# Convolutions of a wavelet block as split float32r products, with weights streamed in pages and shifted copies made by DMA

## What is computed

```python
def conv_block(x):                        # x: group-normalised, one channel per group
    LL, LH, HL, HH = dwt_haar(x)          # four bands of 64 x 64
    hf = concat([LH, HL, HH])             # 96 channels
    x1 = lrelu(conv5(lrelu(conv5(hf, w15)), w25))
    x2 = lrelu(conv3(lrelu(conv3(hf, w13)), w23))
    x3 = lrelu(conv2(lrelu(conv2(hf, w12)), w22))
    y = x1 + x2 + x3
    for w in (wd1, wd2, wd3):
        y = lrelu(conv3(y, w, dilation=2))
    phf = sigmoid(conv1(y, wca)) * hf
    z = batchnorm(conv3(concat([LL, phf]), wcb))
    return idwt_haar(z * sigmoid(z), conv1(phf, whf), HL, HH)

x = x + conv_block(gn(x))
x = x + codebook[argmin(distance(gn(x), codebook))]   # 512 codes of 32 channels
```

## Time and profile before

| | |
|---|---|
| median of 3 runs | 2165.28 us (2164.94 to 2166.05) |
| span of the profiled execution | 2164.4 us |
| TensorE busy, share of the span | 1984.8 us, 92% |
| VectorE busy | 1810.3 us, 84% |
| GpSimd busy (rough) | 1252.3 us, 58% |
| ScalarE busy | 1059.2 us, 49% |
| granted TensorE clock, mean | 0.951 of full speed |

### The profile page before, as it was taken

The page is one execution under the profiler, slowest core; times in us unless marked ns, Lnnn a source line. Parts: engine busy times, 40 slices in busy tenths (PEclk is TensorE's granted clock), DMA queues, the critical chain, the costliest instruction groups (busy, mean ns, idle before and its releaser), DMA issues. The chain is left out here.

```text
span 2164.4 us, 27115 instructions
## 1 busy us (share of the span) xinstructions
PE 1984.8 (92%) x5232; PEld 946.5 (44%) x5232; DVE 1810.3 (84%) x3979; ACT 1059.2 (49%) x2018; POOL 1252.3 (58%) x1299
## 2 busy tenths in 40 slices
PE   6999999999999999999999999999999999995653
PEld 3444455444544455444544445444544445442221
DVE  4122799988999799988999899988999889888996
ACT  5134645545555545546556454546455454543331
POOL 2001277654776377663776367673776457673876
PEclk9999999999999999999999999999999999995555
DMA  6000011111110112111111111111111011110111
GB/s 203 15 10 5 20 40 43 27 29 34 46 35 21 41 36 47 25 24 41 42 36 26 42 35 41 30 24 37 43 41 26 20 25 34 30 25 20 34 37 32
DMA packets 80459, 76.97 MB, mean 36 GB/s; under 512 B 29200, under 2 KB 62608, under 8 KB 80016
## 3 DMA queue, kind: packets, MB, share of 16 engines
q1 hardware_dynamic: 45776, 50.78, 8.3%
q0 software_dynamic: 32768, 16.84, 5.2%
q10 hardware_dynamic: 1728, 7.41, 0.9%
HBM read 41.36 MB, written 16.78 MB: 27 GB/s over the span
## 5 line engine op out<-in xcount | busy, mean ns | idle before, releaser
L1053 POOL DMA_INDIRECT vqc<-in_codebook,idx x1024 | 1000.9, 977 | 545.2 <-DVE idx L964 306.4
L542 PE MATMUL ring<-hf,w_sb 128*128 128x512 f32 x1824 | 888.5, 600 | 2.9 <-ACT hf L715 2.9
L487 PE MATMUL score<-cst,yst 98*128 98x512 f32 x1024 | 788.4, 777 | 83.8 <-DVE idx L964 54.8
L960 DVE MAX8 top<-score 128x8 f32<-128x512 f32 x1024 | 695.3, 684 | 74.7 <-PE score L487 63.8
L964 DVE FIND_INDEX8 idx<-top,score 128x8 uint32<-128x512 f32 x1024 | 704.2, 690 | 0.0
L666 ACT CAST yst<-bands 32x256 fp32r<-32x256 f32 x1024 | 411.3, 402 | 174.6 <-PE score L487 162.1
L542 PEld LDWEIGHTS ring<-hf,w_sb 128*128 128x128 f32 x1824 | 341.6, 191 | 316.9 <-issue 294.2
L487 PEld LDWEIGHTS score<-cst,yst 98*128 98x128 f32 x1024 | 204.0, 202 | 395.0 <-DVE idx L964 206.3
L542 PE MATMUL ring<-ha,w_sb 128*128 128x512 f32 x704 | 347.5, 598 | 5.1 <-DVE ha L853 4.6
L542 PE MATMUL ring<-hb,w_sb 128*128 128x512 f32 x544 | 262.6, 595 | 6.8 <-DVE hb L866 6.8
L627 ACT ACTIVATE z<-ring,prm 128x512 f32<-128x512 f32 x144 | 99.0, 688 | 273.3 <-PE ring L542 272.7
(11 more groups left out here) (101 smaller groups left out, 1276.8 us busy)
## 6 DMA issues: line engine op xcount, KB each, us to landing
xnat<-in_x SPq DMA_DIRECT2D x128, 128.0 KB, 2.7
yst<-yl SPq DMA_DIRECT2D x512, 32.0 KB
vqc<-in_codebook,idx POOLq DMA_INDIRECT x1024
out<-vqc SPq DMA_DIRECT2D x128, 128.0 KB
w_sb<-in_weights ACTq DMA_DIRECT2D x1, 1920.0 KB, 8.2
w_sb<-in_weights ACTq DMA_DIRECT2D x3, 384.0 KB, 12.8
w_sb<-in_weights ACTq DMA_DIRECT2D x1, 1152.0 KB, 15.6
w_sb<-in_weights ACTq DMA_DIRECT2D x1, 960.0 KB, 8.6
```

The source lines that it names most:

```text
L487: nc.tensor.matmul(score[BANK["tile", t]][:, :], yst[0:KST, j % 2, g, wp], cst[0:KST, :], start=True, stop=True).then_inc(s_tile, 1)
L542: t = nc.tensor.matmul(ring[g % RING][:, :, :], w_sb[:, SLOTS[n, m, kind, ky], :], own(source(n, m, kind), half, slice(PAD + di, PAD + di ...
L960: nc.vector.max(top8[:, t % 4, :], score[BANK["tile", t]][:, :]).then_inc(s_top, 1)
L1053: nc.gpsimd.indirect_dma_start(vqc[:, c % 2, w * CH:(w + 1) * CH], None, codebook[:, :], bass.IndirectOffsetOnAxis(idx[:, c % 2, k, 0:1], ...
```

## The change

1. Each product becomes three float32r matmuls. Weights and data are both held as a rounded part and the rest: `MAIN` is rounded by rounded, `WLOW` the rest of the weights by rounded data, `XLOW` rounded weights by the rest of the data. An image takes 678 of them instead of 226.
2. Both parts of 113 matrices don't fit, so they lie in DRAM (`wparts`) in 15 pages of at most 8 matrices (about 1 MB with both parts), and SyncE reads them into a ring of three pages in each round. In the first round they are made: SyncE reads a raw page, ScalarE rounds it, VectorE subtracts, SyncE stores it.
3. Each activation tile gets two parts. The leaky ReLU of w15, w13, w12 and wd1 to wd3 stays in `z`, and the sum behind w22 in `br`. ScalarE copies them rounded (14 copies a round, 128 x 512), and GpSimd subtracts to get the rest (14 subtractions, `split_low`). ScalarE's evacuation waits for VectorE's leaky ReLU in between, and for GpSimd's subtraction of two groups before. The bands are rounded by ScalarE (`normal_own`) with VectorE making the rest (`normal_low`, `ll_low`).
4. `attend` writes the weighted bands to `br`, after each half; ScalarE then scales and rounds (`weighted_high`, directly behind its evacuation of the group), and VectorE makes the rest (`weighted_low`).
5. All shifted copies (`edge`, `side`) are DMAs issued by SyncE, both parts in one DMA, two to four DMAs a copy. ScalarE's copies go.
6. The chunk of the next image is read with even and odd columns apart (runs of 128 bytes), and TensorE makes transpose and Haar transform in one, by four float32 matmuls of 256 columns against a matrix of signs. ScalarE copies to the bands and squares with a sum for the variance; VectorE's four additions and statistics per chunk go.
7. The plan counts 682 steps. `mean2` stands at step 36, `var2` at 60, `bias2` at 72; turns begin at step 84 and end 64 before the end; each of four places (behind w22, wd1, wd2, wd3) counts as 24 places, so that some five turns gather there. A gather is issued a tile later than before. SyncE walks the plan as the others do.

The diff's core:

```diff
-LEAD, REAR = 9, 16
+LEAD, FIRST_TURN, REAR = 36, 84, 64
+CHAIN = ("w22", "wd1", "wd2", "wd3")
+CHAIN_STEPS = 24
+PG, NR = 8, 3
...
+def unit_steps(unit):
+    steps, rest = [], list(unit)
+    while rest:
+        page = PAGE[rest[0]][0]
+        part = [x for x in rest if PAGE[x][0] == page]
+        rest = rest[len(part):]
+        for half in range(2):
+            for terms in ((MAIN, WLOW), (XLOW,)):
+                steps += [("mm", n, half, m, kind, ky, term) for n, m, kind, ky in part for term in terms]
+    return steps
...
+    last = {x[1]: i for i, x in enumerate(plan) if x[0] == "mm"}
+    chained = {last[n] + 1 for n in CHAIN}
+    places = []
+    for i in range(FIRST_TURN, len(plan) - REAR):
+        places += [i] * (CHAIN_STEPS if i in chained else 1)
...
+            def page(b, p):
+                page_freed(sp, b, p - NR)
+                n = len(PAGE_SLOTS[p])
+                sp.dma_start(wring[:, p % NR, :, 0:n, :].bitcast(F32), wparts[:, p, :, 0:n, :]).then_inc(s_page[p % NR], 16)
...
+            def plain_edges(b, n):
+                sp.wait_ge(s_lo, NPART * b + PART[n, 1] + 1)
+                at, done = (0, s_ea) if n in EA else (1, s_eb)
+                for p, src, dst in EDGES:
+                    sp.dma_start(blocks(edge[:, at], p, dst), blocks(SPLIT_TILE[n], p, src)).then_inc(done, 16)
...
             def xchunk(b, k, bank):
-                pe.wait_ge(s_xord, XCHUNKS * b + k + 1)
-                transpose4(score[bank], lambda n: xord[:, k % 2, n * P:(n + 1) * P], s_xT)
+                pe.wait_ge(s_x[k % 2], 64 * ((XCHUNKS // 2) * b + k // 2 + 1))
+                for j in range(2):
+                    for w in range(2):
+                        t = nc.tensor.matmul(score[bank][:, j * 2 * P:(j + 1) * 2 * P], xnat[:, k % 2, w, j * P:(j + 1) * P],
+                                             haar[:, w].rearrange("p e s i -> p (e s i)"),
+                                             start=(w == 0), stop=(w == 1))
...
-                t = nc.tensor.matmul(ring[g % RING][:, :, :], w_sb[:, SLOTS[n, m, kind, ky], :],
-                                     own(source(n, m, kind), half, slice(PAD + di, PAD + di + ROWS)),
+                t = nc.tensor.matmul(ring[g % RING][:, :, :], wring[:, p % NR, int(term == WLOW), at, :],
+                                     own(source(n, m, kind, low), half, slice(PAD + di, PAD + di + ROWS)),
                                      start=(i == first), stop=(i == last))
...
                 if n in LEAKY:
                     wait(act, s_leaky, len(LEAKY) * 2 * b + g - 1)
+                    done = [PART[k] for k in PART if k[0] != "w22" and GROUP[k] <= g - 2]
+                    if done:
+                        act.wait_ge(s_lo, NPART * b + max(done) + 1)
                     nc.scalar.activation(z[:, g % 2], bank[:, :, :], ACT.Identity, bias=col("b" + n[1:]))\
                         .then_inc(s_free, 1)
...
+                    elif n in SPLIT:
                         act.wait_ge(s_leaky, len(LEAKY) * 2 * b + g + 1)
+                        nc.scalar.copy(own(SPLIT_TILE[n][:, 0], half), z[:, g % 2]).then_inc(s_hi, 1)
...
+            def weighted_high(b, par, m, half):
+                act.wait_ge(s_q, 6 * b + 2 * m + half + 1)
+                nc.scalar.activation(own(hf[:, m, 0], half), br[m][:, half * HALF:(half + 1) * HALF, :],
+                                     ACT.Identity, bias=0.0, scale=scale1[par][:, :]).then_inc(s_ph, 1)
...
+            def weighted_low(b, par, m, half):
+                dve.wait_ge(s_ph, 6 * b + 2 * m + half + 1)
...
+            def split_low(b, n, half):
+                g = GROUP[n, half]
+                src = br[0][:, half * HALF:(half + 1) * HALF, :] if n == "w22" else z[:, g % 2]
+                pool.wait_ge(s_hi, NPART * b + PART[n, half] + 1)
+                nc.gpsimd.tensor_tensor(own(SPLIT_TILE[n][:, 1], half), src, own(SPLIT_TILE[n][:, 0], half),
+                                        ALU.subtract).then_inc(s_lo, 1)
...
+            def attend(b, par, m, half):
+                js = slice(half * HALF, (half + 1) * HALF)
+                pool.wait_ge(s_free, NG * b + GROUP["wca", m, half] + 1)
+                nc.gpsimd.tensor_tensor(br[m][:, js, :], raw(par, BANDS[m])[:, js], br[m][:, js, :], ALU.mult)\
+                    .then_inc(s_q, 1)
```

707 lines of the change are left out of this document (424 added, 283 removed).

## The result

| | before | after |
|---|---|---|
| median | 2165.57 us (2164.94 to 2166.05, 4 runs) | 2510.97 us (2510.68 to 2511.31, 4 runs) |
| span of the profiled execution | 2164.4 us | 2508.5 us |
| TensorE busy | 1984.8 us, 92% | 1969.8 us, 79% |
| VectorE busy | 1810.3 us, 84% | 1796.3 us, 72% |
| GpSimd busy (rough) | 1252.3 us, 58% | 1377.9 us, 55% |

The changed kernel takes 1.159 times as long as the one before (95% interval 1.158 to 1.161). The forecast was 2151, its range ended at 2255, and slower had 0.41: the forecast was wrong, in sign and in size. No engine works longer than before but GpSimd, and every engine stands longer.

A forecast was written before the change was run, and what follows sets the result against it. TensorE was taken to bound the steady round (235 of 245.6 us), VectorE and GpSimd close behind. Start 40 + round 0 210 + 7 x 242.1 + last round 205 = 2149.7, forecast 2151 us, range 2045 to 2255.

The forecast's parts named there:

- Rival 4: Stationary loads don't hide: 0.11 us more, 0.33 a matmul, 299 us a round, 2624 us in all; chance 0.04.
- The product: Three float32r matmuls at 0.222 us replace one float32 product: 150.5 against 194.4, 44 us off TensorE per round.
- rival 3: Each float32r matmul costs the score's 0.24 us: 251 us a round, 2226 us in all; chance 0.10.
- Rival 2: The chain loses TensorE's clock, 1.2 against 2.4 GHz, in C and D: round 258 us, 2262 in all; chance 0.22.
- round 0: First round, without tiles to hide the chain: 172.7 us of TensorE work plus stalls, 210 us, as before.
- C: Stage w22 to wd3, 126 matmuls and 40 tiles: 63.8 us, GpSimd's; 6.6 more for tiles gathered before wca.
- D: Stage wca: 6.6 us for tiles gathered before it plus 17.3 for six groups, together 24 us.
- the ring: In wca, ScalarE evacuates, GpSimd attends, ScalarE rounds, then evacuates the next: 2.9 us a group, 17.3 for six.
- E: Stage wcb and whf to the last tile, 66 matmuls and 13.5 tiles: 20 us, TensorE's.
- A: Round's start, 84 matmuls without tiles: 18.6 us plus 3 for the statistics, 21.6 us.
- B: Rest of w15 to w23, 324 matmuls and 66.2 tiles: TensorE 97.7, VectorE 94.3, GpSimd 98.7, so 98.5 us.
- The start: Time before the first product: 40 us (bounds 32 and 50), against 30.3 before.

The follow-up runs named there:

- e4: Changed kernel with the score matmul of each tile gathered behind w22 and wd1 to wd3 issued four times: 2653.2 us, 1.161 of the kernel before.
- e12: Changed kernel with WLOW and XLOW matmuls left out, save those that start, end or signal, waits kept: 2375.0 us, 1.097 of the kernel before.
- e13: Changed kernel with mean2, var2, bias2 and the first turn moved back by 24, 18, 18 and 20 steps: 2620.0 us, 1.159 of the kernel before.
- e9: Changed kernel with wd1 to wca reading the third band's tile (chain cut) and tiles spread evenly: 2409.7 us, 1.113 of the kernel before.
- e10: Changed kernel with wd1 to wca reading the third band's tile (chain cut), tiles still gathered: 2489.3 us, 1.150 of the kernel before.
- e3: Changed kernel with wca's weighted_high and weighted_low issued a group later: 2581.7 us, 1.130 of the kernel before.
- e15: Changed kernel, wca rounding a group later, fewer gathered tiles, later turns and statistics, third page split behind the last image chunk: 2546.6 us, 1.126 of the kernel before.

## Why the prediction was wrong

**The frame, the last round, the loads: right.** The last round is 205.0 as said. Loads of stationary operands hide: had each cost its 0.11, matmuls would stand 0.33 apart, and they stand 0.232 to 0.246. Rival 4 falls. The rule of the Trainium skill that stood beside it (TensorE: Matmul & The Clock Gate, Part 3, What overlaps and what doesn't) isn't borne out for these matmuls. Groups of the page for the new operations answer:

```profile
L1050 DVE SCALAR_TENSOR_TENSOR hf<-br,scale,hf 128x512 fp32r<-128x512 f32 x48 | 36.1, 752 | 155.3 <-ACT hf L875 155.3
...
L1317 POOL TENSOR_TENSOR ha<-z,ha 128x512 fp32r<-128x512 f32 x64 | 70.5, 1101 | 135.9 <-ACT ha L858 135.3
```

`weighted_low` 0.75 (taken 0.83), `split_low` 1.10 (1.11), VectorE's round 220 (222): the operations were sized rightly.

**The product: the upper end, not 0.222.** A mean of 0.241 is rival 3. On 678 products it is 13 us a round where TensorE sets the pace. "Long runs of one type" was an argument without a row; the score's 0.24 was the row that I had. At full clock the products thus give 31 us a round, not 44; the chunk, 1.54 from start to start, was even less than the 1.7 taken. But 87 products a round stood over 0.3 apart, which takes 15 us back, and TensorE's busy time of a round came to 235 in the mean instead of some 205, nearly the 237 of before. The 44 us off TensorE, from which everything else was worked out, were not there.

**Half clock.** Rival 2's condition came true: a clock of 0.87 in a steady round against the 1.00 of the earlier trace rows, with some 440 products of rounds 1 to 7 0.43 apart. Its other sign stayed away: TensorE waited 29 us for DMAs into `edge`, half of that in round 0. Its price, +16 a round in C and D, is not shown either: of the 15 us that the products at a lower clock take from TensorE, 7 lie in C and the ring, and e4, with a higher clock in C, won nothing. Another part lies behind the wait for the statistics, in stage A:

```profile
849.85 8.70 PE L774 MATMUL ring<-hf,wring 128*128 128x512 f32 x36
867.29 0.56 PE L684 MATMUL score<-mv,gmean 128*128 128x1 f32 x2 [8.73 <-DVE mv L1121]
```

```profile
866.88 0.26 DVE L1121 BATCH_NORM_AGGREGATE mv<-st 128x2 f32<-128x24 f32 x1 [7.17 <-issue]
```

The 24 products that follow take 875.55 - 867.71 = 7.84, 0.33 each: 2 us. In E some 20 products a round stand at the lower clock, behind the ring: 3.5 us.

**A, forecast 21.6, was 31.7.** I hid the chain from head to first score under 48 matmuls, but put the head itself at the start of the stage. VectorE reaches mv 10 us after w15 has begun, since `lower_bands` of the last group comes first; in rounds 3 and 5 another 7.2 us, which the profile puts down to issue, stand before it, as shown above. TensorE, through its 36 products in 8.7, waits 8.7 in round 3 and 1.7 in round 4, 24.9 in the seven rounds. From mv to the first score I took 14.1; it was 16.8 in round 3 and 20.1 in round 4, where at the end TensorE waits 3.8 us for the stacking DMAs. e12 and e13 bear it out: A takes 31.7 us with 84 products, 33.2 with 104 (e13), and 32.8 in e12, where most of them are gone.

**B, 98.5, was 108.5.** 324 x 0.019 = 6.2 by the pace, and some 4 us of waits for the stacking DMAs and banks. I had GpSimd and TensorE level here; TensorE filled it (busy 103 of 107.5 in round 3), but e12 shows that the next limit is no more than 4 us lower, so level was not far off.

**C, the step that I trusted least, was 85.7 for 70.4.** The failed step is "I take in each stage the slowest of" TensorE, VectorE and GpSimd. It takes engines as if they had an endless queue between them. Here there are four banks, filled in the order of one list: at a gathering TensorE stands for VectorE, in the burst behind it VectorE stands for TensorE, and the stage takes longer than either engine alone. PE waits 24 us a round in C and DVE 17. e9 and e10 show the price of the gathering, 11.5 a round. How the rest of C's 15 us splits is open. The prediction named the outcome ("all engines idle together and the round is longer than any of my sums"), with ScalarE or SyncE late as its cause, and gave it no time and no chance.

**The ring, 17.3, was 22.5.** 2.9 us a group was the ring without a tile between (2.7 measured); with a tile in it, search and gather join it, 5.9. At its end wcb's first product waits for the ring's banks, 13.5 us in nearly every round; this wait lies inside the 22.5. E itself, +7, is something else: 3.7 us of waits, nearly all for one bank whose search stands behind `weighted_low`, 3.5 for products at the lower clock, and the pace. e3, with a ring 7.5 us shorter, had an E of 28.7 against 27.8 in e4.

**Round 0.** The chain's stalls were sized well: 19 + 3.5 + 3 forecast without the ring, 27 measured by cutting it (231.5 - 204.6). The rest of the miss is the pace (678 x 0.019 = 13) and a clock of 0.91.

**The start, 48.2 for 40.** The order of ScalarE's list, which I had not walked:

```profile
38.14 1.04 ACT L837 CAST wring<-ync 128x1024 fp32r<-128x1024 f32 x1 [8.43 <-DMA ync<-in_weights]
```

The split of the third page waits for its DMA, and the copies of the last two image chunks stand behind it though their transposes are done. e15, with the split behind them, starts the products at 44.4.

**The sum of chances.** Rivals 2 and 3 were both true in their conditions. I gave each its own time and none to both together, nor to a coupling of engines in C. That is how 2511 could lie 256 us over the range with each part only mildly off.

## What to carry over

A sum of "the slowest engine of each stage" is a lower bound, not a forecast. When two engines are each some 75% busy or more and pass work through a few buffers in a fixed order, look for pairs of waits that name each other (here 195 and 142 us in seven rounds): most of what an engine gains there it waits. Before crediting a saving, ask which stages that engine fills alone; here 98 us of TensorE's matmuls a round were worth 13.5. Operations moved into the only path between two convolutions (a split on GpSimd, a DMA, a second pass of ScalarE) are paid for by what is put there to hide them.
